# CIN recommender kernel on one core: a tenth unit split on GpSimd in three rounds of four, the last reads of layer 1 spread over the next round, two units of two late rounds left in full precision

## What is computed

```python
e = jnp.stack([tbl_f[ids[:, f]] for f in range(39)], axis=1)      # (1024, 39, 16)
for i, (W, b) in enumerate(((W0, b0), (W1, b1), (W2, b2))):
    z = jnp.einsum('bfd,bgd->bfgd', x, h)                         # x = e; h = e at first
    cur = relu(jnp.einsum('bfgd,fgl->bld', z, Wr) + b)            # L = 128
    if i != 2: h, direct = cur[:, :64], cur[:, 64:]
    else: direct = cur
z = concatenate(direct parts).sum(-1)
h = relu(concatenate([z, dense_ctx]) @ W_top1 + b_top1)           # (272, 512)
h = relu(h @ W_top2 + b_top2); y = h @ W_top3                     # (512, 256), (256, 1)
```

## Time and profile before

| | us |
|---|---|
| median of three runs | 1286.15 (1285.22 to 1287.26) |
| profiled execution | 1286.31 |
| its span, first to last instruction | 1284.2 |
| busy: PE / VectorE / ScalarE / GpSimd | 1215.5 / 1113.8 / 816.4 / 1036.5 |

### The profile page before, as it was taken

The page is one execution under the profiler, slowest core; times in us unless marked ns, Lnnn a source line. Parts: engine busy times, 40 slices in busy tenths (PEclk is TensorE's granted clock), DMA queues, the critical chain, the costliest instruction groups (busy, mean ns, idle before and its releaser), DMA issues.

```text
span 1284.2 us, 14380 instructions
## 1 busy us (share of the span) xinstructions
PE 1215.5 (95%) x4180; PEld 767.5 (60%) x4180; DVE 1113.8 (87%) x1274; ACT 816.4 (64%) x1115; POOL 1036.5 (81%) x629
## 2 busy tenths in 40 slices
PE   0598999999999999999999999999999999999899
PEld 0254566666666666666666666666666666766545
DVE  2189999999999999999999999999999999999753
ACT  1147566666676667666676667666666778777553
POOL 7458888888988888888988888888988778888733
PEclk9999999999999999999999999999999999999999
DMA  8193466655555566655555666655455665654100
GB/s 185 24 230 93 108 143 147 146 134 116 111 125 119 132 146 147 146 130 115 112 123 122 135 146 147 147 123 118 113 117 123 139 144 144 142 119 118 33 1 1
DMA packets 102510, 156.17 MB, mean 122 GB/s; under 512 B 20811, under 2 KB 32988, under 8 KB 102322
## 3 DMA queue, kind: packets, MB, share of 16 engines
q1 hardware_dynamic: 92256, 152.56, 50.2%
q0 software_dynamic: 10176, 2.70, 2.1%
HBM read 151.31 MB, written 6.19 MB: 123 GB/s over the span
## 4 chain that ended last, share of the span: by engine, by line
PE 80%; DVE 7%; issue 4%; POOL 4%; ACT 4%; DMA 0%; another core or an unknown queue 0%; DVEq 0%; ACTq 0%; POOLq 0%
PE curM L987 36%; PE curM L1004 13%; PE curM L1012 13%; PE curM L1005 13%; DVE z L618 4%; POOL emb L348 3%; ACT h L850 2%; PE xk L976 2%; DVE zl L705 1%; ACT zh L816 1%; DVE zl L696 1%; POOL zl L359 1%; DVE curY L684 1%; DVE z L669 0%; PE h L1110 0%
## 5 line engine op out<-in xcount | busy, mean ns | idle before, releaser
L359 POOL TENSOR_TENSOR zl<-z,zh 128x1024 fp32r<-128x1024 f32 (+1 forms) x301 | 718.4, 2396 | 146.9 <-ACT zh L816 131.0
L618 DVE TENSOR_TENSOR z<-xr,h 128x1024 f32<-128x1024 f32 x456 | 548.4, 1212 | 3.8 <-issue 3.1
L987 PE MATMUL curM<-z,wf 128*128 128x512 f32 (+3 forms) x1220 | 537.4, 600 | 1.0 <-ACT h L850 0.9
L816 ACT ACTIVATE zh<-z 128x1024 fp32r<-128x1024 f32 (+1 forms) x320 | 337.8, 1056 | 291.1 <-DVE z L618 150.6
L348 POOL DMA_INDIRECT emb<-in_tbl_dram,idx x312 | 311.5, 998 | 89.7 <-issue 54.5
L1004 PE MATMUL curM<-zh,wl 128*128 128x512 f32 (+1 forms) x816 | 374.9, 459 | 4.8 <-issue 3.2
L987 PEld LDWEIGHTS curM<-z,wf 128*128 128x128 f32 (+3 forms) x1220 | 214.7, 188 | 237.6 <-issue 217.2
L1005 PE MATMUL curM<-zh,wh 128*128 128x512 f32 (+1 forms) x816 | 321.4, 394 | 0.0
L1012 PE MATMUL curM<-zl,wh 128*128 128x512 f32 (+1 forms) x816 | 255.5, 394 | 9.6 <-POOL zl L359 5.1
L850 ACT ACTIVATE h<-curM,bias 64x512 f32<-64x512 f32 x372 | 240.4, 646 | 20.0 <-DVE z L618 9.9
L696 DVE TENSOR_TENSOR zl<-curY,zh 128x512 fp32r<-128x512 f32 x240 | 164.9, 687 | 71.0 <-ACT zh L801 69.1
(11 more groups left out here) (140 smaller groups left out, 391.0 us busy)
## 6 DMA issues: line engine op xcount, KB each, us to landing
xr<-xT SPq DMA_DIRECT2D x384, 192.0 KB
xs<-xT SPq DMA_DIRECT2D x279, 156.0 KB
xq<-xT SPq DMA_DIRECT2D x64, 256.0 KB
emb<-in_tbl_dram,idx POOLq DMA_INDIRECT x312
xs<-xT SPq DMA_DIRECT2D x62, 78.0 KB
xT<-xc SPq DMA_DIRECT2D x31, 78.0 KB
xr<-in_L_rec_W_dram SPq DMA_DIRECT2D x16, 144.0 KB
xT<-xc SPq DMA_DIRECT2D x31, 40.0 KB
```

Of the source, the lines that this page charges most:

```text
L359: nc.gpsimd.tensor_tensor(zl[0:n, SNUM[r, u] % NL, :], z[0:n, z_slot(r, u), :], zh[0:n, SNUM[r, u] % NH, :], ALU.subtract).then_inc(lo_poo ...
L618: return nc.vector.tensor_tensor(z[:, slot, :].rearrange("p (a n) -> p a n", a=2), x, h, ALU.mult)
L816: nc.scalar.activation(zh[0:n, SNUM[r, u] % NH, :], z[0:n, z_slot(r, u), :], ACT.Copy).then_inc(hi_ready, 1)
L987: mm = nc.tensor.matmul(cur[:, :], wf[rows, full_at(u), a, :], z[rows, z_slot(r, u), a * N:(a + 1) * N], start=start and i == 0, stop=stop ...
```

## The change

Four edits. Unit 4 becomes a G unit in rounds 3 to 24 except those with r%4 of 2, which makes 17 rounds; its split weights are made in round 1. Units 8 and 19 of rounds 29 and 30 are F again. The reads of `take1` at the end of round 29 are moved: the direct half behind unit 18 of round 29, the six reads in pairs behind units 0, 1 and 2 of round 30. Indices of the late weights move up by one.

```diff
-LATE = LATE_C + LATE_A
+TENTH = 4
+LATE = (TENTH,) + LATE_C + LATE_A
+SHORT, LONGER = (STEPS - 3, STEPS - 2), (8, 19)
 LATE_FROM = 25
...
 def kind(r, u):
+    if r in SHORT and u in LONGER:
+        return "F"
+    if u == TENTH and 3 <= r < LATE_FROM and r % 4 != 2:
+        return "G"
...
-                    if r == LATE_FROM and 2 <= u < 2 + len(LATE):
-                        weight_lo_late(u - 2)
+                    if (r, u) == (1, 2):
+                        weight_lo_late(0)
+                    if r == LATE_FROM and 2 <= u < 1 + len(LATE):
+                        weight_lo_late(u - 1)
...
-                    if r == LATE_FROM and 2 <= u < 2 + len(LATE):
-                        weight_hi_late(u - 2)
+                    if (r, u) == (1, 2):
+                        weight_hi_late(0)
+                    if r == LATE_FROM and 2 <= u < 1 + len(LATE):
+                        weight_hi_late(u - 1)
...
-                    if u == UNITS - 1 and (r == -1 or STEPS - 4 < r <= STEPS - 2):
+                    if r == STEPS - 3 and u == C_END - 2:
+                        take1(r, DIRECT)
+                    if r == STEPS - 2 and u < 3:
+                        for i in range(2 * u, 2 * u + 2):
+                            take1(r - 1, i)
+                    if u == UNITS - 1 and r in (-1, STEPS - 2):
                         for i in DIRECT_FIRST:
                             take1(r, i)
...
-                        if r <= LATE_FROM + 1:
+                        if r <= LATE_FROM + 1 and (u != TENTH or r < 6):
                             pe.wait_ge(w_hi, HI_OPS + w + 1)
                             pe.wait_ge(w_lo, LO_OPS + w + 1)
```

## The result

| | before, us | after, us |
|---|---|---|
| median of four runs | 1286.31 (1285.22 to 1287.26) | 1276.51 (1274.37 to 1277.53) |
| profiled execution | 1286.31 | 1275.78 |
| its span | 1284.2 | 1274.0 |

The ratio is 0.9918, with a 95% interval of 0.9904 to 0.9931: faster by 9.8 us between the medians, where 7.4 were forecast. (Ratios are given as recorded, with their intervals.

A forecast was written before the change was run, and what follows sets the result against it. PE's cadence of about 36.2 us a round bounds rounds 2 to 24, VectorE's chain round 30. Savings 5.9 - 0.5 + 2.0 = 7.4 us off a 1284.2 us span, plus 2.1 outside it, gave 1278.9; range 1277.0 to 1283.3.

The forecast's parts named there:

- Unit 4 on PE: Unit 4 split in rounds 3 to 24: 0.35 us saved a round, 17 x 0.35 = 5.9 us.
- The reads of layer 0: PE's unit 10: last read ends at 14.07, its weight load comes at 14.25; cost 0.03 a round, 0.5 us in all.
- same place, and slower: Rival at unit 10: ACT's added copy makes reads 0.9 us late, rounds 0.55 longer, 1293.7 us; chance 0.03.
- Layer 1 at unit 20: Reads end at 28.45 in changed rounds, PE's unit 20 starts at 29.54; 1.1 us left, cost 0.
- GpSimd: One more subtraction a changed round; tightest at unit 7 after a round with r%4 of 3, 0.4 us left, cost 0.
- GpSimd late: Rival: GpSimd's instructions take 4% more and PE waits at unit 7, 6 us lost, 1280 to 1285; chance 0.06.
- last rounds without gain: Rival: `take2` holds the reads up more, or PE's 0.7 us comes through in the last rounds, 1281; chance 0.10.
- a change that does nothing: Rival: the change does not do what it says; excluded by the order of instructions.
- GpSimd beside VectorE: VectorE's products, reading h from PSUM, are not slowed by added GpSimd subtractions; cost 0, against up to 41 us if blocked.
- The last rounds: Full units and moved reads in rounds 29 and 30: tower starts 2.0 us earlier, between 1.6 and 3.0.
- The sum of the direct parts: VectorE's `sum_direct` at unit 3 of round 30 moves by 0.4 us, between 0 and 1.0.
- a better end of round 30: Case in which the end of round 30 gains more than summed, 1277; chance 0.03.

The follow-up runs named there:

- e_act_after: Changed kernel with two idle ACT instructions ahead of the last read of layer 0 in the 17 rounds: 1281.21 us, ratio 0.9994.
- before: The kernel before the change, as profiled in group 1: 1286.31 us.
- before_again: The kernel before, word for word, run again with its own profile in group 5: 1281.25 us, ratio 0.9998.
- e_tail: Kernel before with the edits of the last rounds but not the unit 4 edit: 1277.20 us, ratio 0.9965.
- e_reads: Kernel before with only the reads of layer 1 spread over round 30, all units still split: ratio 0.9983.
- e_full: Kernel before with only units 8 and 19 of rounds 29 and 30 full, reads at the round's end: ratio 0.9963.
- e_only19: Kernel before with one edit, unit 19 of round 30 in full precision: 1278.30 us, ratio 0.9977.
- e_act_before: Kernel before with two idle ACT instructions ahead of the last read of layer 0 in the same 17 rounds: 1281.81 us, ratio 1.0001.
- e_weights: Kernel before with only larger late weight tiles and unit 4's split weights made in round 1, no unit split or moved: 1281.87 us, ratio 0.9996.
- e_all: Changed kernel with unit 4 split also in rounds with r%4 of 2, 22 rounds in all: 1273.79 us, ratio 0.9934.
- e_both: Changed kernel with `take2` of round 29 moved to unit 3 of round 30 and unit 14 split in rounds 6, 10, 14, 18, 22: 1274.90 us, ratio 0.9916.
- e_tenth: Kernel before with the unit 4 edit alone, last rounds as before: 1274.52 us, ratio 0.9944.
- e_warm: Changed kernel with four more matmuls ahead of the picking ones in the start-up: 1275.01 us, ratio 0.9948.

## Why the prediction was right, and where it was wrong

**Unit 4 on PE: right.** 0.35 us in each of 17 rounds: rounds 3 and on take 35.83 to 35.89, those with r%4 of 2 still 36.16 to 36.20. Sum 6.03 in the two profiles of group 1, 5.94 alone, for 5.9.

**The reads of layer 0: right in place, 0.5 us charged too much.** Forecast 14.07, measured 14.08; loads forecast at 14.10, measured at 14.11, and 0.31 long. The cost was 0. The margin behind it was smaller than the 0.18 us reckoned (14.25 less 14.07): `e_act_after` lost the full 0.55 that was added. The rival "same place, and slower" was as near as it was said to be, and its rule, a microsecond of round for each of lateness, was right (0.56 for 0.55); its own case, 0.9 us of lateness, was not run.

**Rounds 25 to 28: no term, 0.29 measured.** The other end of the same margin is seen in round 28 of the kernel before, where the read came at 14.34 instead of 14.07 and the round took 34.95 instead of 34.67. There ACT's half copy ahead of unit 6 starts at 3.38 instead of 3.10, while PE's matmuls up to that place agree to 0.01 us. It is no scatter. All six profiles of kernels whose list of ACT up to round 28 is that of the kernel before have 34.95 (`before`, `before_again`, `e_tail`, `e_reads`, `e_full`, `e_only19`); all thirteen with an instruction added ahead of it have 34.65 to 34.68, even where that instruction is idle (`e_act_before`) or makes weights that nobody uses (`e_weights`). So the gain comes with the change, but not from the unit that it splits. Why is open.

**Layer 1 at unit 20: right.** The reads end at 28.43 (forecast 28.45) and unit 20 starts at 29.55 (29.54): 1.1 us left.

**GpSimd: right.** The tightest place is unit 7 of the rounds with r%4 of 0, PE's need at 10.99 was forecast as 10.98, and the margin is 0.66 us for 0.4 forecast. `e_all` and `e_both` show how near the edge is. Of the rivals, GpSimd late, last rounds without gain and a change that does nothing are out: the first by the absence of a wait of PE for GpSimd, the second by `e_tail`, the third by `e_tenth`.

**GpSimd beside VectorE: right.** The products' mean is 1212 ns over the whole changed kernel, with 17 subtractions more on GpSimd, as before:

```profile
L628 DVE TENSOR_TENSOR z<-xr,h 128x1024 f32<-128x1024 f32 x456 | 548.7, 1212 | 3.8 <-issue 3.1
```

The Trainium skill ("SBUF — State Buffer", Who interferes with whom) says that a VectorE instruction with at most one SBUF input, as this one with its h in PSUM, does not contend with GpSimd; the trace agrees.

**The last rounds: right in sum, 2.14 for 2.0, and in its parts.** The sum of the direct parts moved by 0.52 (0.4 forecast; the prediction's own terms for ACT add up to 1199.96 and not to 1200.1, which gives 0.56), the end of round 30 by 1.62 (1.6 forecast). What the prediction missed is that one of the two edits works against the other. It reckoned both together against the kernel before, and never the full units without the spread reads; so it could not say what each is worth.

**What the range left out.** The forecast was 1278.9, the median 1276.51. Of these 2.4 us, 0.5 is the charge for the reads, 0.1 each unit 4 and the last rounds, 0.3 round 28, and 0.34 the time outside the span. The prediction kept that at 2.1 us; it is 2.07 in the profile of the kernel before and 1.73 in that of the changed one. That is no scatter either. In the timed runs it is 1.68 to 1.81 us in every run of every kernel in which some unit's precision was changed, 2.00 to 2.13 in every run of those in which none was (`e_reads` and `e_act_before` among them), and 1.90 to 1.99 in `e_weights`. I did not find what sets it.

The last 1.0 is the largest step that failed. The prediction had no term for the clock: it took the 2.0 us at the end of round 30 as all that a full unit 19 gives, and then moved one profiled execution, "2.1 us more than its span and 0.2 more than the median", as if it stood for the median in every part. It did not. The profile of before has no clock step in the tower, but the latest start-up of all profiles, 81.53; its total met the median because, as I infer from `e_only19`, the median run before has about 0.8 us of clock step in the place of a part of that start-up. With unit 19 full the changed kernel has no such step in any profile, a gain that a profile without one cannot show. The other 0.2 to 0.3 us is scatter of the start-up as far as is known: in groups 4 and 5 the medians lie 9.4 and 9.3 us apart and not 9.8. The row that pointed to the clock was there, the 0.93 us of idle time ahead of the tower; the prediction gave it no term. The range went below the forecast only for "a better end of round 30", to 1277.0; with 0.8 us for the clock it would have begun at 1276.2 and held the 1276.51.

## What to carry to other kernels

Price a pair of edits against each other and not only against the kernel before: moving reads into the next round cost 1.1 us once full units had already emptied the queue that the reads stood in. Where a chain is held by one read, push that read later by half a microsecond in both kernels: it told in one comparison that the margin was gone in one (0.56 us lost for 0.55 added, 17 times) and at least that wide in the other. And where timed runs spread in steps, look for idle time of PE ahead of a dense stretch: filling it with the slower form of a unit's matmuls saved 2.76 us in the median, where the trace without a clock step shows 2.0. Last, an added instruction can move time in a place that it has nothing to do with, here 0.28 us in round 28; a kernel with the preparation alone (`e_weights`) or with idle work (`e_act_before`) shows it.

## What the runs showed of the hardware

The granted clock of TensorE can fall to its half level behind idle pieces of 0.31, 0.69 and 0.93 us, and does so only in some executions of the same program. It was 1.00, 0.66 or 0.54 of full over the next 5 us after the same 1.92 us of idle time. The timeline of PE in `before_again` shows the price:

```profile
1228.22 0.70 PE L1104 MATMUL h<-dT,xs 16*128 16x512 f32 x2 [0.93 <-ACT h L850]
...
1229.29 5.35 PE L1110 MATMUL h<-zs,xs 128*128 128x512 f32 x8
```

In the changed kernel:

```profile
1224.43 3.70 PE L1127 MATMUL h<-zs,xs 128*128 128x512 f32 x8
```

Over the 5 us after that, all of them filled with matmuls, the clock of `before_again` is back at 1.00. The Trainium skill ("TensorE: Matmul & The Clock Gate", Part 1) says that activity releases the throttle, and that the same kernel meets the gate at another phase from run to run. The traces agree with the first, and with the second in so far as the levels differ while the idle time is the same to 0.01 us; the phase itself no run here shows.

The start-up of the same program differs by about 5 us between groups of runs, 75.5 to 76.9 against 79.8 to 81.5 (`e_warm` apart). It goes with ACT's wait ahead of its first copy of x, 1.24 us against 2.8 to 4.3. What it waits for there, the profile mostly does not name; the data that it copies were ready 1.7 to 3.2 us before in these profiles.
